# One token half at a time: the plain and the weighted up products of a gated expert layer paired, two units together

## The reference, cut to what matters

```python
def _L2_ffn_ref(x, gate_w, gate_b, w1, w2, w3):
    logits = jnp.einsum('bsd,de->bse', x, gate_w) + gate_b
    probs = jax.nn.softmax(logits, axis=-1)
    top_probs, top_idx = jax.lax.top_k(probs, 2)
    top_probs = top_probs / jnp.sum(top_probs, axis=-1, keepdims=True)
    dispatch = jnp.sum(jax.nn.one_hot(top_idx, n_experts, dtype=x.dtype) * top_probs[..., None], axis=-2)
    h1 = jnp.einsum('bsd,edh->bseh', x, w1)
    h2 = jnp.einsum('bsd,edh->bseh', x, w2)
    hidden = jax.nn.silu(h1) * h2
    expert_out = jnp.einsum('bseh,eho->bseo', hidden, w3)
    return jnp.einsum('bseo,bse->bso', expert_out, dispatch)
...
    x = x + _L2_conv_ref(_ln_c(x), L2_conv_W, L2_conv_bias)
    t = _to_tokens(x)
    t = t + _L2_ffn_ref(_ln_t(t), L2_ffn_gate_w, L2_ffn_gate_b, L2_ffn_w1, L2_ffn_w2, L2_ffn_w3)
```

## Time and profile before

| | |
|---|---|
| time, median of 3 runs | 894.55 us (893.32 to 900.33) |
| the profiled execution | 893.4 us, span of its instructions 891.5 us |
| PE busy | 779.4 us, 87% of the span |
| DVE, POOL, ACT busy | 502.2, 424.8, 398.8 us |
| third expert layer, first up product to last down product | 529.8 to 739.2 us |

### The profile page before, as it was taken

One profiled execution on the slowest core, in us unless ns is written; L12 is line 12 of the kernel. 1 busy time (PEld: TensorE's weight loads), 2 busy tenths in 40 slices (PEclk: granted clock), 3 DMA queues, 4 the chain that ended last, 5 costly groups with the idle time before them and its releaser, 6 DMA issues.

```text
span 891.5 us, 16275 instructions
## 1 busy us (share of the span) xinstructions
PE 779.4 (87%) x5575; PEld 377.2 (42%) x5575; DVE 502.2 (56%) x1792; ACT 398.8 (45%) x742; POOL 424.8 (48%) x549
## 2 busy tenths in 40 slices
PE   5777689998899999887878899898999999898896
PEld 2322322345566666662226763232332326553231
DVE  5999866535455554545764554666465455445553
ACT  2001066644355555435454453453343334656563
POOL 2667456664233333413568835544635452106544
PEclk9999989999899999977799989999999999969999
DMA  9610033320000000002350013222222300002334
GB/s 183 112 35 9 13 99 98 99 93 1 3 1 2 3 2 2 3 1 89 129 164 5 1 57 113 80 85 65 97 86 83 94 15 2 1 6 91 106 96 135
DMA packets 48692, 52.55 MB, mean 59 GB/s; under 512 B 18832, under 2 KB 27172, under 8 KB 48612
## 3 DMA queue, kind: packets, MB, share of 16 engines
q1 hardware_dynamic: 47588, 50.46, 20.0%
q0 software_dynamic: 1024, 1.05, 0.6%
HBM read 49.78 MB, written 1.70 MB: 58 GB/s over the span
## 4 chain that ended last, share of the span: by engine, by line
PE 58%; DVE 15%; POOL 9%; issue 9%; ACT 4%; DMA 2%; SPq 1%; POOLq 0%; DVEq 0%; ACTq 0%
PE ps L692 18%; PE ps L697 11%; PE ps L1223 5%; DVE best L392 3%; PE ps L1268 3%; DVE code L395 3%; PE ps L1218 2%; PE ps L1122 2%; PE ps L620 2%; POOL rstd L1563 2%; PE ps L1191 2%; DVE work L941 1%; ACT work L815 1%; PE ps L1832 1%; POOL xn L1573 1%
## 5 line engine op out<-in xcount | busy, mean ns | idle before, releaser
L697 PE MATMUL ps<-work,down 128*64 128x512 f32 x576 | 158.0, 628 | 12.3 <-POOL work L1064 8.8
L692 PE MATMUL ps<-xT,wall 64*128 64x512 f32 x576 | 163.7, 650 | 2.6 <-DVE code L395 1.5
L941 DVE TENSOR_TENSOR work<-aq,ps 128x512 f32<-128x512 f32 x128 | 82.2, 684 | 96.0 <-PE ps L692 91.4
L815 ACT ACTIVATE work<-ps,b1t 128x512 f32<-128x512 f32 x160 | 100.3, 684 | 75.5 <-PE ps L692 75.3
L1057 POOL TENSOR_TENSOR work<-xT,cwb 128x512 f32<-128x512 f32 x64 | 81.3, 1273 | 90.8 <-PE ps L692 76.1
L810 ACT ACTIVATE aq<-ps 128x512 f32<-128x512 f32 x128 | 69.5, 595 | 121.9 <-PE ps L692 121.9
L1076 POOL TENSOR_TENSOR work<-work 128x512 f32<-128x512 f32 x56 | 71.1, 1269 | 63.3 <-DVE work L967 61.7
L692 PEld LDWEIGHTS ps<-xT,wall 64*128 64x128 f32 x576 | 52.1, 197 | 100.1 <-issue 97.2
L967 DVE SCALAR_TENSOR_TENSOR work<-ps,b1t,cwb 128x512 f32<-128x512 f32 x64 | 47.9, 748 | 66.4 <-PE ps L697 47.8
L692 PE MATMUL ps<-work,wall 64*128 64x512 f32 x256 | 72.6, 644 | 10.4 <-DVE work L941 5.3
L283 PE MATMUL ps<-mt,xf 128*128 128x512 f32 x128 | 63.7, 622 | 16.7 <-DVE code L395 16.2
(11 more groups left out here) (229 smaller groups left out, 1397.4 us busy)
## 6 DMA issues: line engine op xcount, KB each, us to landing
cwb<-weight_rows SPq DMA_DIRECT2D x320, 128.0 KB, 3.0
wall<-in_L_ffn_w_dram SPq DMA_DIRECT2D x4, 512.0 KB
wall<-in_L_ffn_W_dram SPq DMA_DIRECT2D x4, 256.0 KB
out_dram<-tokens SPq DMA_DIRECT2D x8, 128.0 KB, 2.5
tokens<-in_x_dram SPq DMA_DIRECT2D x1, 896.0 KB, 6.4
ak<-in_L_conv_emb_dram SPq DMA_DIRECT2D x2, 256.0 KB, 3.5
zq<-in_L_conv_emb_dram,code POOLq DMA_INDIRECT x32, 2.4
down<-in_L_ffn_W_dram SPq DMA_DIRECT2D x2, 256.0 KB
```

The costliest lines, as they stand in the source:

```text
L692: ins = pe.matmul(m.ps[:, bank + half, :], m.wall[r, at + g * P:at + (g + 1) * P], x[r, :], start=True, stop=True)
L697: ins = pe.matmul(m.ps[half * C:half * C + C, bank, :], m.down[l][:, n % G, :], m.hid[:, n % 3, half, :], start=start, stop=True, skip_gro ...
L815: act.activation(m.hid[:, n % 3, half, :], m.ps[:, 2 * (n % 2) + half, :], ACT.Gelu, bias=bias)\
L941: dve.tensor_tensor(m.hid[:, n % 3, half, :], m.silu[:, n % 2, half, :], m.ps[:, 2 + half, :], ALU.mult)\
```

## The change

A unit's four up products are paired in another way. `both(n, half)` takes one token half: its plain product on that half of the rows, and its weighted product on the other half of the rows, side by side, into one pair of banks. There are three pairs of banks (0 and 1, 2 and 3, 4 and 5), used in turn by u = 2n + half. For that the weighted inputs must lie with their halves exchanged: SP copies `xT` crosswise to `xTs` by two DMAs for each block (`exchange`, semaphore `f_xs`), and `share` fills the weights crosswise too. POOL's `scale_inputs` reads `xTs` in place of `xT`.

PE takes two units together: the eight up products of units i+2 and i+3, `extras(i)`, down of i, `extras(i+1)`, down of i+1. A pair waits for its `xs` ahead of its plain product as well. Silu and gate follow pair by pair (`f_h2` counts pairs), `hid` becomes `hid4` with four buffers, and DVE's order becomes `gate(i+2)`, `extras(i)`. `WHEN` and the orders on ACT and POOL stay.

```diff
@@ -570,9 +571,20 @@
         for half in range(2):
-            sp.dma_start(slot[half * C:half * C + C, :], rows[half * E + n % G].partition_broadcast(C)).then_inc(landed, 16)
+            at = (1 - half) * C if f["gated"] else half * C
+            sp.dma_start(slot[at:at + C, :], rows[half * E + n % G].partition_broadcast(C)).then_inc(landed, 16)
+
+    def exchange(sb):
+        sp.wait_ge(s.f_xt, S0 + sb + 1)
+        if sb > 1:
+            sp.wait_ge(s.f_pw, p0 + (sb - 1) * G)
+        for half in range(2):
+            at = (1 - half) * C
+            sp.dma_start(m.xTs[at:at + C, sb % 2, :], m.xT[half * C:half * C + C, sb, :]).then_inc(s.f_xs, 16)
 
     def write(sb):
+        if f["gated"]:
+            exchange(sb)
         sp.wait_ge(s.f_cwt, S0 + sb + 1)
@@ -692,9 +704,23 @@
+    def both(n, half):
+
+        u = 2 * n + half
+        at, r, other = 2 * (u % 3), slice(half * C, half * C + C), slice(C - half * C, P - half * C)
+        g = n % G * P
+        pe.wait_ge(s.f_xt, S0 + n // G + 1)
+        pe.wait_ge(s.f_pw, p0 + n + 1)
+        if u > 2:
+            pe.wait_ge(s.f_hw, d0 + u - 2)
+        pe.matmul(m.ps[:, at, :], m.wall[r, w["up"] + g:w["up"] + g + P], m.xT[r, n // G, :], start=True, stop=True)
+        pe.matmul(m.ps[:, at + 1, :], m.wall[other, w["up2"] + g:w["up2"] + g + P], m.xs[other, n % 2, :],
+                  start=True, stop=True).then_inc(s.f_h2, 1)
...
-    def second(n):
-        if n >= U:
-            return
-        pe.wait_ge(s.f_pw, p0 + n + 1)
-        if n > 0:
-            pe.wait_ge(s.f_hw, d0 + 2 * n)
-        up(n, w["up2"], 2, s.f_h2, m.xs[:, n % 2, :])
@@ -748,21 +761,26 @@
-    first(0)
-    first(1)
     if f["gated"]:
-        second(0)
-    for i in range(U):
-        if f["gated"]:
-            second(i + 1)
-        first(i + 2)
-        extras(i)
...
+        for i in range(-2, U, 2):
+            for n in (i + 2, i + 3):
+                if n < U:
+                    both(n, 0)
+                    both(n, 1)
+            for n in (i, i + 1):
+                if n >= 0:
+                    extras(n)
+                    down_gated(n)
@@ -802,12 +820,15 @@
             if f["gated"]:
-                if n > 1:
-                    act.wait_ge(s.f_hw, d0 + 2 * (n - 2) + half + 1)
-                act.activation(m.silu[:, n % 2, half, :], m.ps[:, 4 * (n % 2) + half, :], ACT.Silu).then_inc(s.f_silu, 1)
+                u = 2 * n + half
+                act.wait_ge(s.f_h2, u + 1)
+                if u > 3:
+                    act.wait_ge(s.f_hw, d0 + u - 3)
+                act.activation(m.silu[:, n % 2, half, :], m.ps[:, 2 * (u % 3), :], ACT.Silu).then_inc(s.f_silu, 1)
@@ -933,12 +954,12 @@
-        dve.wait_ge(s.f_h2, n + 1)
-        if n > 2:
-            dve.wait_ge(s.f_yps, u0 + n - 2)
+        if n > 3:
+            dve.wait_ge(s.f_yps, u0 + n - 3)
         for half in range(2):
-            dve.wait_ge(s.f_silu, 2 * n + half + 1)
-            dve.tensor_tensor(m.hid[:, n % 3, half, :], m.silu[:, n % 2, half, :], m.ps[:, 2 + half, :], ALU.mult)\
+            u = 2 * n + half
+            dve.wait_ge(s.f_silu, u + 1)
+            dve.tensor_tensor(m.hid4[:, n % 4, half, :], m.silu[:, n % 2, half, :], m.ps[:, 2 * (u % 3) + 1, :], ALU.mult)\
                 .then_inc(s.f_hw, 1)
@@ -996,13 +1017,14 @@
         gate(0)
+        gate(1)
     for i in range(U):
...
             if f["gated"]:
-                gate(i + 1)
+                gate(i + 2)
@@ -1051,10 +1073,10 @@
         pool.wait_ge(landed, count)
-        pool.wait_ge(s.f_xt, S0 + n // G + 1)
+        pool.wait_ge(s.f_xs, 32 * (n // G + 1))
         if n > 1:
-            pool.wait_ge(s.f_h2, n - 1)
-        pool.tensor_tensor(m.xs[:, n % 2, :], m.xT[:, n // G, :], slot, ALU.mult).then_inc(s.f_pw, 1)
+            pool.wait_ge(s.f_h2, 2 * (n - 1))
+        pool.tensor_tensor(m.xs[:, n % 2, :], m.xTs[:, n // G % 2, :], slot, ALU.mult).then_inc(s.f_pw, 1)
```

More of the change, by code:

```diff
@@ L493 @@
 UNITS_BEFORE = before(UNITS)
+UPS_BEFORE = before([0 if f["gated"] else u for f, u in zip(FFN, UNITS)])
 GELU_BEFORE = before([0 if f["gated"] else 2 * u for f, u in zip(FFN, UNITS)])
@@ L641, in ffn_pe @@
     E = f["E"]
-    u0, g0, d0, p0, y0 = UNITS_BEFORE[l], GELU_BEFORE[l], DVE_BEFORE[l], POOL_BEFORE[l], YT_BEFORE[l]
+    g0, d0, p0, y0 = GELU_BEFORE[l], DVE_BEFORE[l], POOL_BEFORE[l], YT_BEFORE[l]
     tokens, logits, weights = ffn_pe_routing(pe, m, s, l)
@@ L693, in up @@
         ins.then_inc(sem, 1)
+    def both(n, half):
[9 more added lines that the diff above has]
+                  start=True, stop=True).then_inc(s.f_h2, 1)
     def down(n, bank, start):
         for half in range(2):
-            ins = pe.matmul(m.ps[half * C:half * C + C, bank, :], m.down[l][:, n % G, :], m.hid[:, n % 3, half, :],
+            hid = m.hid4[:, n % 4, half, :] if f["gated"] else m.hid[:, n % 3, half, :]
+            ins = pe.matmul(m.ps[half * C:half * C + C, bank, :], m.down[l][:, n % G, :], hid,
                             start=start, stop=True, skip_group_check=True)
@@ L704, in first @@
         pe.wait_ge(s.f_xt, S0 + n // G + 1)
-        if f["gated"]:
-            if n > 1:
[L707 to L712, removed]
-    def second(n):
-        if n >= U:
-            return
-        pe.wait_ge(s.f_pw, p0 + n + 1)
-        if n > 0:
-            pe.wait_ge(s.f_hw, d0 + 2 * n)
-        up(n, w["up2"], 2, s.f_h2, m.xs[:, n % 2, :])
+        if n > 1:
+            pe.wait_ge(s.f_hid, g0 + 2 * (n - 1))
+        up(n, w["up"], 2 * (n % 2), s.f_hps, m.xT[:, n // G, :])
     def down_apart(n):
@@ L749, in down_gated @@
         down(n, 6, n % G == 0)
-    first(0)
-    first(1)
     if f["gated"]:
-        second(0)
-    for i in range(U):
-        if f["gated"]:
-            second(i + 1)
-        first(i + 2)
-        extras(i)
[L760 to L765, removed]
+        for i in range(-2, U, 2):
[7 more added lines that the diff above has]
+                    down_gated(n)
+    else:
+        first(0)
+        first(1)
+        for i in range(U):
+            first(i + 2)
+            extras(i)
+            if POST[l]:
+                down_apart(i)
+            else:
+                down_weighed(i)
     return lambda: back(SUPERS - 1, 7 if f["gated"] else 6)
@@ L804, in unit @@
             return
-        act.wait_ge(s.f_hps, u0 + n + 1)
+        if not f["gated"]:
+            act.wait_ge(s.f_hps, UPS_BEFORE[l] + n + 1)
         for half in range(2):
             if f["gated"]:
-                if n > 1:
-                    act.wait_ge(s.f_hw, d0 + 2 * (n - 2) + half + 1)
-                act.activation(m.silu[:, n % 2, half, :], m.ps[:, 4 * (n % 2) + half, :], ACT.Silu).then_inc(s.f_silu, 1)
+                u = 2 * n + half
[3 more added lines that the diff above has]
+                act.activation(m.silu[:, n % 2, half, :], m.ps[:, 2 * (u % 3), :], ACT.Silu).then_inc(s.f_silu, 1)
             else:
@@ L2130, in program @@
         m.hid = work[:, 0:6 * 512].rearrange("p (a h n) -> p a h n", a=3, h=2)
+        m.hid4 = work[:, 0:8 * 512].rearrange("p (a h n) -> p a h n", a=4, h=2)
         m.part = work[:, 6 * 512:8 * 512].rearrange("p (k n) -> p k n", k=2)
@@ L2144, in program @@
         m.emb = m.ak[:, 2:4, :, :].rearrange("p r g n -> p (r g n)").rearrange("p (k a c) -> p k a c", a=2, c=C)
+        m.xTs = m.ak[:, :, :, :].rearrange("p r g n -> p (r g n)")[:, 0:2 * 512].rearrange("p (k n) -> p k n", k=2)
         m.silu = m.aq[:, :, :, :].rearrange("p r g n -> p (r g n)").rearrange("p (k h n) -> p k h n", k=2, h=2)
```

2 lines of the change are left out of this document (1 added, 1 removed).

## The result

The changed kernel took 916.62 us in the median of four runs (914.5 to 921.8), the kernel before 896.58 (893.3 to 900.3); the ratio is 1.021, with a 95% interval of 1.018 to 1.025. The forecast was 910.2 us, in a range of 899 to 923. The profiled execution took 915.7 us, with a span of 913.8.

The account below looks back on a forecast made before the run. The prediction took PE to bound the kernel, busy for 87% of the span. Its terms, -10.6 + 1.3 + 17.4 + 7.5 = +15.6 us on 894.55, gave 910.2 us, in a range of 899 to 923.

Parts of the forecast that it names:

- The chains through POOL: At round heads PE waits for gate, DVE steps, `scale` and `xs`: waits of 26.3 us in place of 8.9, +17.4.
- four `centre` waits: Behind four of the long waits, `centre` on POOL delays the round's second `xs`: 0.5 us each, 2.0 together.
- two waits put down to `combine`: `combine` of blocks 2 and 3 between two gates, with the exponentials delaying a silu: 1.0 us each, 2.0 together.
- The clock: Behind four waits longer than 2.90 us PE runs at half speed: 6.8 to 13.4 us, taken as +7.5 net.
- Two units together: Two changes of array split per two units, not four: round 5.5 us in place of 5.84, 31 rounds, -10.6 us.
- the rival of the banks: A round's fourth pair waits a quarter microsecond for a late gate: up to +8 us, 918 us; chance 0.12.
- Another pairing: Neighbouring pairs meet with the same half of the rows; taken as free, since row groups start passes independently: 0.
- exchange: Two DMAs and a POOL wait per block, taken as covered ahead of the first use: 0.
- A rule of strict start and end in program order: Rival: products on PE are not reordered, +0.86 us a unit, 53 us in all, 963 us; chance 0.06.
- Start and end: Two more down pairs left at the layer's start, +1.9; last down pair no longer waits, -0.6; together +1.3 us.

Follow-up runs that it names:

- experiment 1: Changed kernel with POOL's nine later normalisation steps one to three units later in POOL's list: 895.9 us, ratio 1.000, layer 206.8 us.
- experiment 7: Changed kernel's pairing, banks and exchange, but one unit at a time, with the old table of steps: 902.7 us, ratio 1.007, layer 216.7 us.
- experiment 4: Changed kernel with unused extra products in PE's waits ahead of units 10, 26, 44, 60, and the bank wait moved ahead: 909.1 us, ratio 1.014.
- experiment 5: As experiment 1, plus silu and gate of each round's first pair done in two halves of 256 columns: 890.2 us, ratio 0.991, layer 204.5 us.
- experiment 3: Changed kernel with the weighted product ahead of the plain one for every second pair: 920.0 us, ratio 1.028, layer 235.3 us.
- experiment 8: Kernel before, plus the two exchange DMAs per block and POOL's wait for them, copy unused: 896.1 us, ratio 0.998, layer 211.3 us.
- experiment 6: Changed kernel with later POOL steps, DVE's and ACT's routing steps behind a round's second unit, SP's weights one unit later: 884.8 us, ratio 0.985.

## Why the prediction was right, step by step

- **The chains through POOL** (+17.4 forecast) carried the result, and experiments 1 and 7 show it. The waits measured ahead of units 10, 26, 44, 60 and 29 are 8.14, 3.99, 3.99, 3.99 and 2.21 us, where 8.1, 3.8, 4.3, 4.3 and 1.8 were forecast. Two terms were mis-sized, in opposite directions, and that they cancel is luck. The four `centre` waits of 0.5 did not show, as PE ran at half speed there; the clock's term had taken them off. And the two waits put down to `combine` of blocks 2 and 3 are 2.02 and 2.03 us, not 1.0 each. The prediction had the wrong step there: the gate that PE waits for stands behind `hits`, at i = 17 and 33; behind `combine` PE waits 0.15 us, once. A cast of `hits` takes 1.20 us in place of 0.17, beside a POOL operation (last section); with 0.17 the gate could have started 1.03 us earlier, as its silu was there, and the wait would be about the 1.0 of the forecast. Together the waits grew by 18.6 us, 0.4 of it at the layer's start, which the last term counts.
- **The clock** (+7.5): the four stretches cost half of the time that PE worked in them, 1.4 + 1.6 + 1.7 + 1.7 = 6.5 us, and a fifth, behind the wait of 2.02 us, some 1.7 (611.40 to 614.81). These are costs beside the waits as they were measured; taking the four stretches away gives back less, 3.4 to 4.2 us by experiment 4. (The prediction's own range of 6.8 to 13.4 has its middle at 10.1, not at the 9.5 that it took.) The prediction had taken 2.27 us as a wait that leaves the clock alone; one of 2.02 did not, and one of 2.03 at 670.64 did. The length of a wait alone does not decide it.
- **Two units together** (-10.6) was the step that failed in size: a quiet round gives 0.21 us, not 0.34. The prediction compared the end of the gate, T + 2.55, with the time when PE wants to start the fourth pair, T + 2.68, and took the margin for enough. The rows show the gate's end at T + 2.56. But a pair's weight load stands behind the same wait, and in the other pairs it runs beside the passes ahead; released this late it does not, and the pair costs 0.13 more. This is the rival of the banks at half its price, and experiment 5 shows it by removing it. By experiment 4, 0.09 of it hangs on the place of that wait among the three that stand ahead of a pair. With some 24 rounds that have it the term is -10.6 + 24 x 0.14 = -7.2.
- **Another pairing** and **exchange** (0 each) were right by experiments 3, 7 and 8. A rule of strict start and end in program order ("TensorE: Matmul & The Clock Gate" of the Trainium skill, Part 3) does not hold for these products on different row groups: a quiet unit of four products in the order upper, lower, lower, upper takes 2.93 us, where the prediction's reading of that rule would add 0.86.
- **Start and end** (+1.3): the fifth pair starts at 541.96, 11.71 us behind the start of the last products of the stage ahead; the weighted pair of unit 2 in the kernel before, 11.98 behind it (539.91 and 527.93). At the end the last down pair follows its neighbour at 0.86, where it was 1.46. That makes -0.3 + 1.9 - 0.6 = +1.0. Nearly right.

The terms as measured, -7.2 + 1.0 + 18.2 + 8.2 = 20.2, stand against 20.4 in the layer and 15.6 in the forecast: 3.4 are missing from the two units, 0.8 from the waits and 0.7 from the clock, less 0.3 at the start. The span grew by 2 us more outside the layer, which is within what that rest differs by between traces. Between the medians of the result the change cost 20.0 us. That the median of 916.6 lies 6.4 above the forecast of 910.2 is for 2.0 us the kernel before, whose median rose from 894.55 to 896.58 with a fourth run.

## What to carry to other kernels

When work on the bounding engine is taken in larger batches, list every side step that stands in a queue between the batch's products and the next batch's inputs, and add up the whole chain from the last product; here a table of due times that was good for one unit at a time cost 25 us with two, and moving entries in it, with SP's weights one unit later, turned 2% slower into 1.5% faster. Put side steps at the end of a batch, where the engine that runs them has its gap. And ask of a buffer that is freed just in time whether the weight load ahead of the product is in time too. Check also what else an edit moves: in experiment 4 the place of one wait was worth 0.09 us in every round.

## What the runs showed of the hardware

Two kinds of DVE operation here last until a POOL operation that was under way at their start has ended; the gates do not. Rows of the changed kernel, POOL's `xs` and a cast of DVE of 128 x 16 elements, and the same cast in experiment 6, where POOL is idle:

```profile
608.31 1.27 POOL L1079 TENSOR_TENSOR work<-ak,cwb 128x512 f32<-128x512 f32 x1 [2.53 <-PE ps L717]
...
608.41 1.20 DVE L900 CAST topf<-topi 128x16 f32<-128x16 uint32 x1
```

```profile
561.91 0.17 DVE L900 CAST topf<-topi 128x16 f32<-128x16 uint32 x1
```

1.20 us and 0.17: the cast ends at 609.61, 0.03 behind POOL's operation. The twelve traces hold 192 casts of this step. The 89 that meet no POOL operation take 0.17 to 0.18 us; of the 91 that start while a tensor operation of POOL is under way, 88 end 0.03 us behind it, with lengths from 0.20 to 1.20 us, and the other three met one that was over within 0.13 us. A subtraction of two SBUF operands shows the same, 0.29 us alone and 1.10 beside `xs` (604.83 to 605.93, POOL 604.51 to 605.78). The gates, with one operand in PSUM, keep 0.69 us beside `xs`. This agrees with "SBUF — State Buffer" of the Trainium skill, section "Who interferes with whom": a DVE instruction with two SBUF inputs, or a cast in a two-port mode, and a POOL instruction that reads SBUF exclude each other for the whole instruction. Whether this cast runs in such a mode no trace shows. No experiment here moved POOL's operation alone, so that 1 us of each of the two waits of 2 us comes from there is worked out from rows, not shown by a run.
